# Perceiver layers on one core: context tiles in groups of eight instead of seven, and in the first attention the projections between the halves of a weighing

## The reference, cut to what matters

```
k = ctx @ Wk.T + bk;  v = ctx @ Wv.T + bv          # both attentions, the same ctx
s = (q / 4) @ k.T  (+ (1 - mask) * -10000 in the first attention)
out = softmax(s) @ v
x = x + attention 0;  linear attention, gelu, ternary FFN;  x = x + attention 1;  RWKV, conv FFN
```

## Time and profile before

| | |
|---|---|
| median of 3 runs | 1016.34 us (1014.98 to 1018.03) |
| the profiled execution, own time | 1017.67 us |
| its span in the trace | 1015.9 us |
| TensorE busy | 975.3 us (96%) |
| VectorE busy | 735.7 us (72%) |
| ScalarE busy | 677.9 us (67%) |
| GpSimd busy | 434.4 us (43%) |

### The profile page before, as it was taken

The page is one execution under the profiler, slowest core; times in us unless marked ns, Lnnn a source line. Parts: engine busy times, 40 slices in busy tenths (PEclk is TensorE's granted clock), DMA queues, the critical chain, the costliest instruction groups (busy, mean ns, idle before and its releaser), DMA issues.

```text
span 1015.9 us, 37764 instructions
## 1 busy us (share of the span) xinstructions
PE 975.3 (96%) x16380; PEld 599.1 (59%) x16381; DVE 735.7 (72%) x1719; ACT 677.9 (67%) x963; POOL 434.4 (43%) x396
## 2 busy tenths in 40 slices
PE   8899999999999999999887899999999999999987
PEld 3356555655565655656563566666666666666666
DVE  5788888888888888887547776655665655666466
ACT  2777887787787878787563556656566665656653
POOL 4369898899888889884100100111111010100000
PEclk9999999999999999999999999999999999999999
DMA  8411122012201222014014001111001111000000
GB/s 325 135 35 54 64 75 73 23 56 75 75 22 56 74 76 67 10 57 165 1 39 159 2 4 37 39 38 39 23 19 38 39 39 39 2 3 3 2 2 5
DMA packets 15829, 53.11 MB, mean 52 GB/s; under 512 B 4400, under 2 KB 6064, under 8 KB 14768
## 3 DMA queue, kind: packets, MB, share of 16 engines
q1 hardware_dynamic: 15664, 50.70, 14.5%
HBM read 50.56 MB, written 0.13 MB: 50 GB/s over the span
## 4 chain that ended last, share of the span: by engine, by line
PE 76%; issue 7%; ACT 6%; DVE 6%; POOL 4%; DMA 1%; SPq 0%; POOLq 0%; DVEq 0%; ACTq 0%
PE ps_out L1418 14%; PE ps_scores L1399 14%; PE ps_proj L1317 13%; PE ps_proj L1332 11%; PE ps_max L1339 7%; POOL probs L514 4%; PE ps_scores L1395 4%; PE ps_scores L1317 3%; ACT probs L681 2%; ACT probs L676 2%; PE ps_scores L1429 1%; ACT probs L669 1%; DVE tile_max L949 1%; DMA bq<-in_L_xattn_bq 1%; PE ps_scores L1332 1%
## 5 line engine op out<-in xcount | busy, mean ns | idle before, releaser
L949 DVE TENSOR_REDUCE tile_max<-ps_max 128x1 f32<-128x448 f32 x339 | 198.7, 619 | 138.3 <-PE ps_max L1339 130.7
L946 DVE CUSTOM_DVE_ANT_0 unread<-ps_max,masks 128x448 bf16<-128x448 f32 x367 | 215.2, 621 | 57.7 <-PE ps_max L1339 56.1
L514 POOL TENSOR_TENSOR probs<-probs,masks 128x512 f32<-128x512 f32 x182 | 229.9, 1285 | 58.5 <-ACT probs L669 57.3
L681 ACT ACTIVATE probs<-ps_scores 128x1024 f32<-128x1024 f32 x193 | 187.3, 1021 | 78.8 <-PE ps_scores L1399 78.7
L676 ACT ACTIVATE probs<-probs 128x1024 f32<-128x1024 f32 x196 | 207.6, 1059 | 37.2 <-DVE probs L1007 28.4
L1399 PE MATMUL ps_scores<-q_pad,k_full 32*128 32x256 f32 x3088 | 230.4, 375 | 0.0
L1418 PE MATMUL ps_out<-probs,values 128*32 128x128 f32 x6272 | 222.1, 278 | 3.5 <-ACT probs L676 3.1
L1418 PEld LDWEIGHTS ps_out<-probs,values 128*32 128x32 f32 x6272 | 157.0, 110 | 63.1 <-issue 44.4
L1399 PEld LDWEIGHTS ps_scores<-q_pad,k_full 32*128 32x128 f32 x3088 | 191.5, 185 | 0.5
L1339 PE MATMUL ps_max<-k_high,q_high 32*128 32x448 bf16 x710 | 162.1, 358 | 7.9 <-DVE tile_max L949 4.4
L1332 PE MATMUL ps_proj<-ctx_t,wk 128*32 128x448 f32 x1552 | 166.2, 546 | 0.2 <-DVE tile_max L946 0.2
(11 more groups left out here) (304 smaller groups left out, 927.4 us busy)
## 6 DMA issues: line engine op xcount, KB each, us to landing
ctx_t<-in_ctx_t SPq DMA_DIRECT2D x27, 896.0 KB, 5.4
masks<-in_mask_n SPq DMA_DIRECT2D x14, 448.0 KB, 3.5
masks<-in_mask_t SPq DMA_DIRECT2D x14, 448.0 KB, 3.6
room_w<-in_L_attn_f_w SPq DMA_DIRECT2D x2, 1024.0 KB, 8.7
room_w<-in_L_ffn_w SPq DMA_DIRECT2D x2, 1024.0 KB, 7.1
room_w<-in_L_ffn_w_gate SPq DMA_DIRECT2D x1, 1024.0 KB, 10.6
room_w<-in_L_ffn_w_up SPq DMA_DIRECT2D x1, 1024.0 KB, 12.8
room_w<-in_L_ffn_w_down SPq DMA_DIRECT2D x1, 1024.0 KB, 14.8
```

The source lines that it names most:

```text
L514: nc.gpsimd.tensor_tensor(p, p, three(mask_t[m % 2], TILES)[:, t, :].unsqueeze(1).to_broadcast([P, 4, P]), ALU.add).then_inc(sig("bias_add ...
L681: nc.scalar.activation(prob(T, half), scores_half(T, half), ACT.Exp).then_inc(sig(f"exp_done{half}"), 1)
L946: ins = v.tensor_tensor_reduce(unread[:, j % 2, :], max_bank(m, j)[:, 0:HALF], mask_n[m % 2][:, HALF * half:HALF * (half + 1)], 1.0, -3e38 ...
L949: ins = v.tensor_reduce(tile_max[:, h, half:half + 1], max_bank(m, j)[:, 0:HALF], AX_X, ALU.max)
```

## The change: what it does

Groups of `GT` = 8 tiles (1024 keys) take the place of blocks of seven; `TILES` is 1 and counts only in the host's layout. An attention has `NG` = 13 groups, twelve of eight tiles and one of two. Maxima products and reads are 512 columns wide (256 in the last group), keys pieces too; values have four pieces of two tiles, all into `ps_proj`, at t = 1, 3, 5, 7. The maxima of a full group stand at two places in a tile only: two behind the scores, two ahead. The sums are turned into `ps_out`.

In the first attention, except where sums are turned and in the "lone" tiles, the projection (and the turned maxima) stand between the two halves of the weighing. ScalarE copies a tile's second scores, then takes the second exponent of the tile before, then this tile's first exponent. The lone tiles, with VectorE adding the mask to both halves, are the last eight instead of the last seven.

```diff
-TILES = 7
+TILES = 1
 KB = TILES * P
 NB = SK // KB
-HALF = KB // 2
+GT = 8
+GK = GT * P
+NG = -(-NB // GT)
+HALF = GK // 2
...
+SPLIT = 4
+LONE_FROM = 2
...
+        def size(m):
+            return min(GT, NB - GT * (m % NG))
...
+        def lone(m, t):
+            return m % NG == NG - 1 or m % NG == NG - 2 and t >= LONE_FROM
+        def lone_at(m, t):
+            return t - LONE_FROM if m % NG == NG - 2 else GT - LONE_FROM + t
+        def spare(m, t):
+            return lone(m, t) and lone_at(m, t) > 0
...
-        SCORED_AT = ((2, 1, 2, 1, 2, 1, 1), (2, 2, 2, 2, 2, 2, 2))
-        WEIGHED_AT = ((0, 2, 0, 2, 0, 2, 2), (0, 2, 0, 2, 0, 0, 0))
...
             elif m == 0:
-                now = (1, 2, 2) if t == WEIGHTS_AT else (2, 2, 2) if t < LAST_AT else (1, 2, 0) if t == LAST_AT else now
-            elif n + 1 < NB and t <= LAST_AT:
-                now = (first, middle, 2 if t < LAST_AT else 0)
-            if n + 2 < NB and m != NB:
-                ahead = (0, 0, 2) if t == LAST_AT else (first, middle, 2) if t > LAST_AT else ahead
+                now = (2, 2, 2) if t < 3 else (2, 0, 2) if t < CHAIN_AT else (2, 0, 0) if t == CHAIN_AT else now
+            elif n + 1 < NG and size(m + 1) < GT:
+                now = ((2, 0, 2), (2, 0, 2), (2, 0, 0))[t] if t < 3 else now
+            elif n + 1 < NG and t <= CHAIN_AT:
+                now = (2, 0, 2 if t < CHAIN_AT else 0)
+            if n + 2 < NG and m != NG:
+                ahead = (0, 0, 2) if t == CHAIN_AT else (2, 0, 2) if t > CHAIN_AT else ahead
             return own, now, ahead
...
                         here = []
                         for to, count in zip((m, m + 1, m + 2), counts):
                             at = done.get(to, 0)
-                            here += [(to, j) for j in range(at, at + count[k])]
+                            upto = min(at + count[k], maxima_of(to)) if count[k] else at
+                            here += [(to, j) for j in range(at, upto)]
                             if count[k]:
-                                done[to] = at + count[k]
-                        swapped = k == 0 and len(here) == 2 and (m == 0 or m >= NB and sum(count[1] for count in counts) == 2)
+                                done[to] = upto
+                        swapped = k == 0 and len(here) == 2 and (m == 0 or m >= NG and sum(count[1] for count in counts) == 2)
                         two = m > 0 and k == 0 and len(here) == 2 and not swapped
                         for i, (to, j) in enumerate(here):
-                            if i == 0 and (two or k == 0 and late_bank(m, t) or len(here) == 3) or i == 1 and swapped:
+                            if i == 0 and two or i == 1 and swapped:
                                 MAX_BANK[to, j] = 2
                             else:
                                 MAX_BANK[to, j], MAX_AFTER[to, j] = turn_of, read[turn_of]
-                                read[turn_of] = 2 * H * to + j + 1
+                                read[turn_of] = maxima0(to) + j + 1
...
-        VALUES_AT = {1: 0, 3: 1, 5: 3}
-        LENT_VALUES_AT = {5: 2}
+        VALUES_AT = {1: 0, 3: 1, 5: 2, 7: 3}
         def tiles_of(u):
-            return (slice(0, 2), slice(2, 4), slice(4, 5), slice(5, 7))[u]
-        CHAIN_AT, ROWS_AT = 5, 6
-        LATE_AT = 4
...
-                            exp_in_place(T, 0)
+                max_out(NG * l)
+                for n in range(NG):
+                    m = NG * l + n
+                    for t in range(size(m)):
+                        T = tile0(m) + t
+                        if l == 0 and lone(m, t):
+                            if not spare(m, t):
+                                exp_in_place(*tile_ahead_of(m, t), 1)
+                            stage_sums(m, t)
+                            exp_in_place(m, t, 1)
+                            exp_in_place(m, t, 0)
                             lent_out(m, t)
                             projected(m, t)
                         elif l == 0:
-                            if rowed(m, t):
-                                rows_out(rowed(m, t))
                             copy_second(T)
                             if T == 0:
                                 abs_sum(2)
+                            else:
+                                exp_in_place(*tile_ahead_of(m, t), 1)
+                            exp_in_place(m, t, 0)
+                            projected(m, t)
+                            lent_out(m, t)
                             stage_sums(m, t)
-                            exp_in_place(T, 0)
-                            lent_out(m, t)
-                            projected(m, t)
-                            exp_in_place(T, 1)
                         else:
-                            exp_scores(T, int(is_last(m)))
-                            exp_scores(T, 1 - int(is_last(m)))
+                            exp_scores(m, t, int(lone(m, t)))
...
+                        if sums_turned_in(m, t):
+                            add_sums(stage(m, t) - 1, ps_out)
+                        if l == 0 and lone(m, t):
                             bias_last(m, t)
                         elif l == 0:
                             bias_first(m, t)
                         for k, j in behind_scores[early:]:
                             maximum(k, j)
-                        if sums_turned_in(m, t) and is_last(m):
...
+            def weigh_half(m, t, half):
+                T, first = tile0(m) + t, int(lone(m, t))
+                if half == first or m < NG or lone(m, t):
+                    pe.wait_ge(sig(f"exp_done{half}"), T + 1)
+                for j, h in enumerate(HEADS[half]):
+                    g, c, o = h % 4, h // 4, place(h)
+                    last = mm(ps_out[VW * g:VW * (g + 1), P * c:P * (c + 1)], values[m % 2][:, t, h, :],
+                              prob(T, half)[:, P * o:P * (o + 1)], start=(in_stage(m, t) == 0 and half == first and j < 4), stop=ends_stage(m, t),
+                              skip_group_check=True)
+                if m < NG and lone(m, t) and half == first:
+                    proj_free(None)
+                    mm(ps_proj[0:32, 0:P], ident[:, 0:32], ident[:, :], start=True, stop=True)
+                return last
...
                             maximum(k, j)
-                        if rowed(m, t) and m < NB:
-                            proj_free(("max_copied", rowed(m, t) + 1))
-                            turn_max(rowed(m, t))
-                        if sums_turned_in(m, t) and is_last(m):
-                            proj_free(("acc_added", stage(m, t)))
-                            turn_sums(stage(m, t) - 1)
-                        if t > 0:
-                            weigh(m, t - 1)
-                        elif n > 0:
-                            weigh(m - 1, TILES - 1)
+                        if sums_turned_in(m, t):
+                            turn_sums(stage(m, t) - 1, ps_out)
+                            projections(m, t)
+                            pe.wait_ge(sig("acc_added"), stage(m, t))
+                        inside = l == 0 and tile0(m) + t > 0 and not lone(m, t) and not sums_turned_in(m, t)
+                        if inside:
+                            def both():
+                                projections(m, t)
+                                rows_turned(m, t)
+                            weigh(*tile_ahead_of(m, t), both)
+                        elif n > 0 or t > 0:
+                            weigh(*tile_ahead_of(m, t))
                         for k, j in behind_weighing:
                             maximum(k, j)
-                        if sums_turned_in(m, t) and not is_last(m):
-                            turn_sums(stage(m, t) - 1, lent(m, t))
                         if (m, t) == (0, WEIGHTS_AT):
                             pe.wait_ge(sig("abs_sums"), 3)
```

461 lines of the change are left out of this document (232 added, 229 removed).

## The result

The changed kernel takes 1044.18 us (median of 4 runs, 1043.45 to 1045.78); the kernel before, on the same chip, 1016.52 us. The ratio is 1.0274, with a 95% interval of 1.0255 to 1.0294: slower by 28 us. The profiled execution took 1045.78 us around a span of 1044.0.

The account below looks back on a forecast made before the run. It took TensorE, 96% busy, as the bound: time falls only if it works or waits less. Terms 16 + 5 + 2.6 + 2.5 + 2.5 - 4.6 - 4 gave +20 on a median of 1016.34: 1036 us, range 1009 to 1048.

Parts of the forecast that it names:

- The wait in a tile: First attention: TensorE stands 0.52 us per tile at the projection for VectorE's third read; a tile takes 4.73 us.
- the wait is not there: Rival for the first attention: the third read ends by 1.88 us, so no wait; 993 us, faster; chance 0.18.
- The group: Full groups of the first attention: 39.2 us against 37.4, +1.8 each, +16 us for nine.
- Sums' tile: First attention's tile that turns the sums: transposes fall under the wait and the weighing is undivided; 5.17 us.
- last tile: Last tile of a first-attention group: turns the maxima inside and waits for ScalarE's late copy of the rows; 5.61 us.
- First group and ahead of it: First group 48.0 us against 41.7, of +6 taken 5; wider keys and one more values tile ahead, +2.6.
- The end of the first attention: The first attention's last 18 tiles: 77.9 us against 75.4, +2.5.
- 4.8 of hand-over and close: Part of the sum for the first attention's last tiles: 4.8 us after the eight tiles with masks on VectorE.
- Between the attentions: Between the two attentions: eight longer paired reads (1.0 us) and some seven keys on the path at 0.2; +2.5.
- Second attention: Whole weighing, wait 0.1, tile 4.24 us; groups 35.2 against 35.8, -4.6 for eight; -4 at its end.
- The late exponent: Rival for the first attention: exp_done1 misses the second half in three tiles a group by 0.5; 1049 us; chance 0.12.
- The rule that wide vector instructions save their fixed part: Skill's rule against the forecast: 96 fewer instructions would give some 12 us of VectorE and 2 of TensorE.

Follow-up runs that it names:

- e9: The changed kernel with VectorE reading only the first 256 of each 512 columns of the first attention's maxima; 1013.92 us.
- e7: The changed kernel with the last group's second key part cast one group earlier and the maxima turned early in the lone tile; 1041.75 us.
- e11: e8 with the last group's second key part cast one group earlier and the maxima turned early in the lone tile; 1007.6 us.
- e2: The changed kernel with ScalarE taking both exponents of a tile in that tile again, TensorE's split weighing kept; 1044.13 us.
- e3: The changed kernel with TensorE's and ScalarE's orders in the first attention both as before, groups of eight kept; 1027.35 us.
- e8: e3 with maxima turned into ps_proj right behind the scores in a first-attention group's last tile, rows copied first, two maxima moved behind the weighing; 1013.31 us.
- e1: The changed kernel with TensorE weighing both halves ahead of the projection again, ScalarE's new order kept; 1138.11 us.
- e5: The changed kernel with one first-attention maximum moved between the weighing's first half and the projection, none going to ps_proj, from the second group on; 1052.98 us.
- e6: The changed kernel with the first group's maxima given the order of the other groups; 1043.01 us.
- e10: e8 with the edits of e6 and e7 added; 1012.36 us.

## Why the prediction was right, and which of its terms were not

It said 1036 us, range 1009 to 1048, slower, by one mechanism; measured 1044.2, by that mechanism, and inside the narrower 1024 to 1046 of the forecast itself. Step by step:

- **The wait in a tile.** Release at +2.40, tile 4.73: measured 2.40 and 4.69. The reads start at 0.42, 1.04 and 1.65, as worked out (0.43, 1.04, 1.66). TensorE arrives at 1.97 instead of 1.88 (234.06 less 232.56, and 0.47), so it stands 0.43 instead of 0.52. What the sum left out is that ps_proj's own product allows a start at 1.61, not 1.53 (1.10 + 0.51, e9), so the queue decided by 0.04 us only. The rival "the wait is not there" was further off than it looked: even reads of 256 columns kept the release at 2.10, behind an arrival of 1.88 (242.79 less 241.38, and 0.47).
- **The group.** Sums' tile 5.17, last tile 5.61, group 39.2: measured 5.14 (91.30 to 96.44), 5.37 and 38.96. The last tile was not over-estimated: the next tile's maxima start without the rows, and the wait for the rows stands in that tile, in front of its scores (0.41 us in the rows below), which makes it 4.97 instead of 4.73; 5.61 + 4.73 and 5.37 + 4.97 are both 10.34. The group is shorter by the 0.04 of each of its five plain tiles. +16 for nine groups was +13.7.

```profile
242.62 0.39 PE L1381 MATMUL ps_max<-k_high,q_high 32*128 32x512 bf16 x2
243.03 0.39 PE L1431 MATMUL ps_scores<-max_rows,minus 32*128 32x512 bf16 x4
```

- **First group and ahead of it.** 48.0 + 2.6: measured 48.2 (38.55 to 86.73) and 2.7. The error is the 41.7 for before, which was 41.0, and the 5 that I took where my own sum gave 6: +7.6 forecast, +9.8 measured.
- **The end of the first attention** is the step that failed most: +2.5 forecast, +7.1 measured. The tiles without a projection cost 4.24 each, with 1.52 us of waiting for the second exponent, near the 4.04 forecast. Not seen were a cast that comes too late for the short last group (1.31) and the hand-over of maxima in the lone tiles (1.41 + 1.17); e7 removed these three, 3.9 us, and took 4.5 us away, the rest with the clock that had fallen behind them. "4.8 of hand-over and close" stood for places that I had not walked through.
- **Between the attentions** +2.5: measured +3.6.
- **Second attention.** Tile 4.24, group 35.2: measured 4.23 (673.81 to 678.03) and 35.23. -8.6 was -6.1. The eight steady groups are 0.5 us shorter each, as forecast to within 0.1; the rest of the difference lies around them, in stretches where I had again estimated tiles instead of following them.

The window of one of its groups, beside the earlier trace rows:

```profile
696.97:732.21 35.24, 35.02 (x650) 21.51 (x649) 20.64 (x36) 21.68 (x27) 4.68 (x7) 1.00 0.10 33
```

The gain or loss of a steady group was right to 0.3 us in either attention. Of the 8 us that the sum was short, the steady groups of the first attention gave back 2; the stretches that occur once were 10 short. The late exponent, a rival with 0.12, showed only in the two tiles without a projection. The rule that wide vector instructions save their fixed part (the Trainium skill, "VectorE: DVE Perf Modes", TRN2 errata) holds for the reads: their instructions, 96 fewer, were busy for 14 us less (567.1 before, 553.1 after, by line), near the 12 us estimated. The other half of VectorE's 28.8 us is not theirs: 10.3 us of it are two small instructions of `chain`, whose mean went from 770 to 432 ns and from 384 to 229 ns. The time went the other way, because the third read ended later and nothing stood in front of the projection any more to cover it.

What the change was worth, part by part: groups of eight with the old orders, with the turned maxima where they used to be and the end's two waits removed, gain 9 us (e11); the projection inside the weighing loses 17 (e2 against e3); ScalarE's order is worth nothing by itself (e2). e3's first group took 44.8 us against 41.0 before; e8 brought it to 41.6. Why the stretch between the attentions is longer than before was not tried.

## What to carry to other kernels

A block of work that covers a wait has a value that no busy share shows: before splitting it, write down when the instruction behind it is released and when the engine would arrive. Count both chains to a release, the queue of readers and the single product with its latency. And cost the stretches that occur once (first group, short last group, hand-over) tile by tile as well, for some 10 of this case's 28 us were there and unforeseen.

## What the runs showed of the hardware

**A small vector instruction waits for a GpSimd instruction to end.** In e3 the `TENSOR_SCALAR` of 128x16 started at 227.11 and took 1.17 us, to 228.28. GpSimd there:

```profile
225.72 2.52 POOL L562 TENSOR_TENSOR probs<-probs,masks 128x512 f32<-128x512 f32 x2
```

which ends at 228.24. At 472.56 in the same trace, with GpSimd idle, it took 0.18 us. Its mean is 813 ns there, 770 ns in the kernel before and 432 ns in the changed one. The Trainium skill, "SBUF — State Buffer", Who interferes with whom, says that VectorE and GpSimd share a pair of ports as an exclusive lock, held for a whole instruction, and counts `tensor_scalar` among those that can want it: the trace agrees, 1.0 us for an instruction of 0.18. In e8 it still takes 1.18 us (at 222.13), and yet the last tile is 1.4 us shorter: what it costs depends on what queues behind it. The reads of maxima, which come from PSUM, kept 0.61 us apart beside GpSimd's adds.

**A stand of TensorE can cost more than its length, but not each time.** In the first tile of the changed kernel TensorE stands 0.96 us, and the keys behind took 3.39 us, the clock being granted at 0.65 from 40 to 44 us. In e7 the code is the same up to there and the stand is 0.97 us, but the clock stays at 1.00 and the keys took 1.93 us. The keys in the two traces:

```profile
41.60 3.39 PE L1374 MATMUL ps_proj<-ctx_t,wk 128*32 128x512 f32 x16 [0.17 <-DVE tile_max L991]
41.59 1.93 PE L1381 MATMUL ps_proj<-ctx_t,wk 128*32 128x512 f32 x16 [0.22 <-DVE tile_max L998]
```

The kernel before (0.90 us, keys 3.21) is like the first; e1, e2, e3, e5 and e8 (0.97 us, keys 1.92) are like the second. Behind a stand of 2.71 us in the same tile the clock was low in both traces that have it (e6 and e10, keys 3.57 and 3.64). Four waits of 0.79 to 0.87 us between 47 and 63 us in the changed kernel had no low clock behind them: it is 1.00 in every window from 48 to 68 us. So some 1.5 us at such a place can be the clock's and not the program's; look at the granted clock before two tiles are compared.
